# Graph network on one core: edge stages with the layer norm on edge partitions, four buffers, sums and transposes three rounds behind

## What is computed

```python
h = relu(layernorm(x)); x = x + degree_scaled_sum(h[src] -> dst)
e = ln(mlp(edge_attr)); n = ln(mlp(relu(layernorm(x))))
for s in range(2):
    e = e + ln(mlp([e, n[senders], n[receivers]]))
    agg = segment_sum(e, receivers)
    n = n + ln(mlp([n, agg]))
return x + mlp(n)
```

## Time and profile before

| | |
|---|---|
| median of 3 executions | 13500.32 us (13497.44 to 13505.08) |
| profiled execution, first to last instruction | 13501.9 us |
| TensorE busy, mean granted clock | 10188.2 us (75%), 0.851 |
| ScalarE / VectorE / GpSimd busy | 7395.3 / 5621.3 / 9021.1 us |

### The profile page before, as it was taken

How to read it: one execution, slowest core, us unless ns; L and a number is a source line. 1 busy time by engine, 2 the same in 40 slices (tenths; PEclk the granted TensorE clock), 3 DMA queues, 4 the chain that set the end, 5 groups by cost and what they waited for, 6 DMA issues and landing times. The chain is left out here.

```text
span 13501.9 us, 245430 instructions
## 1 busy us (share of the span) xinstructions
PE 10188.2 (75%) x61106; PEld 7311.0 (54%) x61106; DVE 5621.3 (42%) x18295; ACT 7395.3 (55%) x11725; POOL 9021.1 (67%) x9433
## 2 busy tenths in 40 slices
PE   4877777777777777777777777777777777777777
PEld 3655555555555555555555555554555555555554
DVE  5653333333333334444444444443444444444443
ACT  0025555555555535666666666665666666666665
POOL 0037777777777736777777777773777777777773
PEclk9986666666666658999999999998999999999998
DMA  2012222222222223333333333332222333333331
GB/s 76 11 27 43 43 43 43 42 43 43 43 43 43 43 33 82 93 94 94 94 94 94 94 94 93 94 94 58 68 68 68 68 68 68 68 69 68 68 69 33
DMA packets 1693848, 867.49 MB, mean 64 GB/s; under 512 B 1234324, under 2 KB 1391253, under 8 KB 1693347
## 3 DMA queue, kind: packets, MB, share of 16 engines
q1 hardware_dynamic: 1390930, 589.01, 16.6%
q0 software_dynamic: 301056, 257.50, 11.7%
q10 hardware_dynamic: 1808, 20.32, 0.5%
HBM read 635.66 MB, written 246.07 MB: 65 GB/s over the span
## 5 line engine op out<-in xcount | busy, mean ns | idle before, releaser
L1151 POOL DMA_INDIRECT edge_blk_g<-sender_part,edge_blk_idx x6272 | 6014.8, 959 | 2441.7 <-issue 1997.8
L892 POOL DMA_INDIRECT fl_g<-sender_x,fl_idx x3136 | 2992.8, 954 | 1025.9 <-issue 992.3
L1203 PE MATMUL edge_blk_hps<-ident,edge_blk_g 128*128 128x128 f32 x6272 | 1081.6, 325 | 1635.5 <-DMA edge_blk_g<-sender_part,edge_blk_idx 1635.3
L1203 PEld LDWEIGHTS edge_blk_hps<-ident,edge_blk_g 128*128 128x128 f32 x6272 | 910.5, 223 | 2284.9 <-DMA edge_blk_g<-sender_part,edge_blk_idx 2284.0
L1231 ACT ACT_TABLE_LOAD x1568 | 2011.7, 1283 | 51.6 <-PEq L66 23.6
L1276 DVE TENSOR_TENSOR edge_blk_t<-edge_blk_yb,edge_blk_rps 128x512 f32<-128x512 f32 x784 | 539.5, 688 | 2420.5 <-PE edge_blk_rps L1167 2420.3
L1237 ACT ACTIVATE edge_blk_h<-edge_blk_hps,vecs 128x512 f32<-128x512 f32 x784 | 538.8, 687 | 1485.5 <-PE edge_blk_hps L1203 1483.1
L1244 ACT ACTIVATE edge_blk_sq<-edge_blk_yps,vecs 128x512 f32<-128x512 f32 x784 | 538.9, 687 | 1388.7 <-PE edge_blk_yps L1211 1384.1
L984 ACT ACTIVATE fl_sq<-fl_yps,vecs 128x512 f32<-128x512 f32 x392 | 269.4, 687 | 1641.2 <-PE fl_yps L947 1641.2
L1308 DVE TENSOR_SCALAR edge_blk_ohb<-row_f,edge_blk_lst 128x64 f32<-128x64 f32 x6272 | 1115.7, 277 | 6.4
L975 ACT ACT_TABLE_LOAD x784 | 1005.9, 1283 | 31.5 <-PEq L66 17.5
(11 more groups left out here) (222 smaller groups left out, 15503.1 us busy)
## 6 DMA issues: line engine op xcount, KB each, us to landing
edge_blk_e<-edge_state SPq DMA_DIRECT2D x784, 256.0 KB
edge_state<-fl_e SPq DMA_DIRECT2D x392, 256.0 KB
edge_blk_dlb<-local_dst SPq DMA_DIRECT2D x1568, 64.0 KB
edge_blk_g<-sender_part,edge_blk_idx POOLq DMA_INDIRECT x6272
edge_state<-edge_blk_new SPq DMA_DIRECT2D x392, 256.0 KB, 2.1
fl_g<-sender_x,fl_idx POOLq DMA_INDIRECT x3136
edge_blk_win<-receiver_part SPq DMA_DIRECT2D x1568, 16.0 KB
fl_attr<-attr_slots SPq DMA_DIRECT2D x392, 32.0 KB
```

The lines of the kernel that those rows point to most:

```text
L892: pool.indirect_dma_start(out=g[n.b][:, j, :], out_offset=None, in_=xg_d, in_offset=bass.IndirectOffsetOnAxis(ap=idx[n.b][:, j:j + 1].bitc ...
L1151: pool.indirect_dma_start(out=g[n.b][:, i, 64 * c:64 * c + 64], out_offset=None, in_=ps_d, in_offset=bass.IndirectOffsetOnAxis(ap=idx[n.b] ...
L1203: ins = nc.tensor.matmul(h_ps[:, P * i:P * i + P], g[n.b][:, i, :], ident[:, :], start=False, stop=i == TILES - 1)
```

## The change

Each edge round keeps its gathers and its three products, and changes what follows `h`:

- `y` is computed with `h` as the stationary operand (`second`), so that the edges lie on partitions. The bias is a row (`b1_row`), added by VectorE (`yb`); ScalarE squares `yb` from SBUF; VectorE reduces, inverts and multiplies. The matmuls `varps` and `rps` and ScalarE's `rs_x`, `yb` and `eb` are gone.
- The sums use the normalized `t` directly. Gain is applied as they are added, and `agg` is not cleared in the edge steps: it carries over, and `agg_w` and a corrected bias of `edge_blk1` carry the gains' and offsets' part for the nodes. The edge state in HBM leaves out the offset in the steps.
- `sums` and `turn` (transposes of `t`; in the first layer by 64-wide matmuls) run three rounds behind, in the first layer four.
- Buffers filled by loads, `t`, `new` and `ohb` are fourfold, PSUM outputs double. Index list and receiver list are one load. `rounds` unrolls four rounds.
- `ohb` is one broadcast `tensor_tensor` and no longer eight `tensor_scalar`; the first layer's `e` is a `tensor_scalar` from PSUM.

The first layer's gathered rows land beside `t` in `gx`, and one set of matmuls sums both (96 columns). The setup gets some sixteen small VectorE operations and eight matmuls. Cut to its core:

```diff
 edge_step, GpSimd:
-  landed(pool, idx_in, n)
-  wait(pool, pre, n.back(2))
+  landed(pool, list_in, n)
+  wait(pool, pre, n.back(4))
 edge_step, VectorE:
-  for j in range(8):
-      ins = v.tensor_scalar(ohb[n.b][:, j, :], row_f[:, 0:WIN], lst[n.b][:, j:j + 1].bitcast(F32), None, ALU.is_equal)
+  v.tensor_tensor(ohb[n.b][:, :, :], row_f[:, 0:WIN].rearrange("p (j w) -> p j w", j=1).broadcast_to([P, 8, WIN]),
+                  lst[n.b][:, 8:16].bitcast(F32).rearrange("p (j w) -> p j w", w=1).broadcast_to([P, 8, WIN]), ALU.is_equal).then_inc(ohb_ok, 1)
-  v.tensor_tensor(t[:, :], yb[n.b][:, :], r_ps[:, :], ALU.mult).then_inc(t_ok, 1)
-  v.scalar_tensor_tensor(new[n.b][:, :], t[:, :], col("g"), eb[n.b][:, :], ALU.mult, ALU.add).then_inc(new_ok, 1)
+def normed(n):
+  wait(dve, y_ok, n)
+  v.tensor_tensor(yb[n.half][:, :, :], y_ps[n.half][:, :].rearrange("p (j d) -> p j d", d=D),
+                  b1_row.rearrange("p (j d) -> p j d", j=1).broadcast_to([P, 8, D]), ALU.add).then_inc(yb_ok, 1)
+  wait(dve, sq_ok, n)
+  v.tensor_reduce(red[:, :], sq[:, :, :], AX_X, ALU.add).then_inc(red_ok, 1)
+  wait(dve, sd_ok, n)
+  v.reciprocal(rs[:, :], sd[:, :]).then_inc(r_ok, 1)
+  wait(dve, r_ok, n)
+  v.tensor_tensor(t[n.b]..., yb[n.half][:, :, :], rs[:, :]...broadcast_to([P, 8, D]), ALU.mult).then_inc(t_ok, 1)
+def finish(n):
+  v.scalar_tensor_tensor(new[n.b][:, :], t_ps[n.half][:, :], col("g"), e[n.b][:, :], ALU.mult, ALU.add).then_inc(new_ok, 1)
+def body(n):
+  one_hots(n)
+  add_sums(n.back(3))
+  finish(n.back(3))
+  normed(n.back(1))
-  v.memset(agg[:, :], 0.0).then_inc(zeroed, 1)
+  for b in range(QUAD):
+      ins = v.memset(win[b][:, :], 0.0)
+  ins.then_inc(zeroed, 1)
 edge_step, TensorE:
+def second(n):
+  wait(pe, h_ok, n)
+  wait(pe, yb_ok, n.back(2))
+  for i in range(TILES):
+      ins = nc.tensor.matmul(y_ps[n.half][:, P * i:P * i + P], h[n.half][:, P * i:P * i + P], w_mid[:, :], start=True, stop=True)
+  ins.then_inc(y_ok, 1)
 def body(n):
+  sums(n.back(3))
+  turn(n.back(3))
+  second(n.back(1))
   ...
 edge_step, ScalarE:
+def body(n):
+  scale(n.back(1))
+  silu(n)
 edge_step, SP:
+def body(n):
+  indices(n)
+  operands(n.back(2))
+  store(n.back(6))
 first_layer, TensorE and VectorE:
+for i in range(TILES):
+  for c in range(2):
+      ins = nc.tensor.matmul(t_ps[n.half][64 * c:64 * c + 64, P * i:P * i + P], gx[n.b][:, i, c, 0:D], ident[:, :], start=True, stop=True)
 def body(n):
-  encode(n.back(1))
-  turn_in(n)
-  spread_out(n.back(2))
-  sums(n.back(2))
-  second(n.back(1))
+  second(n.back(2))
+  encode(n.back(1))
+  turn_in(n)
+  sums(n.back(4))
+  turn(n.back(4))
 def body(n):
+  attr_copy(n)
+  one_hots(n.back(2))
+  normed(n.back(2))
+  add_sums(n.back(4))
+  finish(n.back(4))
 finish(n):
-  v.tensor_scalar(e[n.b][:, :], t[:, :], col("g"), col("beta"), ALU.mult, ALU.add).then_inc(e_ok, 1)
+  v.tensor_scalar(e[n.b][:, :], t_ps[n.half][:, :], col("g"), col("beta"), ALU.mult, ALU.add).then_inc(e_ok, 1)
```

More of the change, by code:

```diff
@@ L835, in first_layer @@
         sem = ctx.enter_context(semaphores(nc, "fl_"))
[L837 to L844, removed]
-        rs_x = two("rs_x", [P, 2 * TILES, D])
-        yb = two("yb", [P, CHUNK])
@@ L847, in first_layer @@
-        idle = sb("idle", [P, 1])
-        e = two("e", [P, CHUNK])
-        at_ps, h_ps, var_ps, agg_ps, r_ps = ps("atps"), ps("hps"), ps("varps"), ps("aggps"), ps("rps")
-        y_ps = [ps("yps0"), ps("yps1")]
-        idx_in, list_in, attr_in, g_in, e_out = ([sem(f"{k}{i}") for i in range(2)] for k in ("idx_in", "list_in", "attr_in", "g_in", "e_out"))
+        lst = many(QUAD, "lst", [P, 16], I32)
+        attr = many(QUAD, "attr", [P, 8, E_DIM])
+        gx = many(QUAD, "gx", [P, TILES, 2, D + XG])
@@ L956, in body, with turn @@
+                def turn(n):
+                    if not n.exists():
+                        return
+                    wait(pe, e_ok, n.back(2))
+                    for i in range(TILES):
+                        for c in range(2):
+                            ins = nc.tensor.matmul(t_ps[n.half][64 * c:64 * c + 64, P * i:P * i + P], gx[n.b][:, i, c, 0:D],
+                                                   ident[:, :], start=True, stop=True)
+                    ins.then_inc(turned, 1)
                 def body(n):
+                    second(n.back(2))
@@ L967, in _ @@
-                second(last.back(1))
-                spread_out(last.back(1))
-                sums(last.back(1))
+                for k in (4, 3, 2, 1):
+                    sums(last.back(k))
+                    turn(last.back(k))
+                    if k == 4:
+                        second(last.back(1))
             @block.scalar
@@ L999, in _ @@
+                last = rounds(act, body, count_sb, 2)
+                scale(last.back(2))
+                silu(last.back(1))
+                scale(last.back(1))
             @block.vector
@@ L1090, in edge_step @@
-        rs_x = two("rs_x", [P, 2 * TILES, D])
-        yb = two("yb", [P, CHUNK])
-        idle = sb("idle", [P, 1])
-        new = two("new", [P, CHUNK])
-        new_t = sb("new_t", [P, TILES, P])
-        y_ps = [ps("yps0"), ps("yps1")]
-        h_ps, var_ps, t_ps, agg_ps, r_ps = ps("hps"), ps("varps"), ps("tps"), ps("aggps"), ps("rps")
-        idx_in, list_in, dlb_in, win_in, g_in, e_in, e_out = (
-            [sem(f"{k}{i}") for i in range(2)] for k in ("idx_in", "list_in", "dlb_in", "win_in", "g_in", "e_in", "e_out"))
+        lst = many(QUAD, "lst", [P, 16], I32)
@@ L1192, in body @@
+                def second(n):
+                    if not n.exists():
+                        return
+                    wait(pe, h_ok, n)
+                    wait(pe, yb_ok, n.back(2))
+                    for i in range(TILES):
+                        ins = nc.tensor.matmul(y_ps[n.half][:, P * i:P * i + P], h[n.half][:, P * i:P * i + P], w_mid[:, :],
+                                               start=True, stop=True)
+                    ins.then_inc(y_ok, 1)
                 def body(n):
-                    wait(pe, h_ok, n.back(1))
@@ L1219, in body @@
[L1219 to L1225 removed]
+                last = rounds(pe, body, count_sb, 2)
+                for k in (3, 2, 1):
+                    sums(last.back(k))
+                    turn(last.back(k))
+                    if k == 3:
+                        second(last.back(1))
             @block.scalar
```

575 lines of the change are left out of this document (280 added, 295 removed).

## The result

The changed kernel takes 13600.13 us (median of 4 runs, 13591.66 to 13606.61) against 13500.01 us of the kernel before (4 runs): ratio 1.0072, 95% interval 1.0058 to 1.0087. It is slower by 0.7%, where 13402 us was forecast.

What follows compares the result with a forecast made beforehand. POOL's gathers with their issue were taken as the bound, 11732 of the loops' 12019 us. Terms -5 - 83 - 25 + 5 + 7 + 3 = -98 us on 13501.9 gave 13404, as median 13402 us; range 13340 to 13500.

Steps and rivals of the forecast that it cites:

- POOL as the bound: In the three loops, POOL's gathers and their issue set the time: 11732 of 12019 us, other engines' work fitting beside them.
- -83: Stretched gathers in the three loops: 35, 28 and 20 us won by the new `ohb` and `fl_e` from PSUM.
- The second rival: New two-input VectorE operations in the loops disturb gathers, 62 ns at each of 2352 places: +145 us, 13547; chance 0.05.
- The first rival: Nothing won on gathers: `oha`, placed elsewhere in VectorE's round, costs what `ohb` cost: 13485 us, no change; chance 0.08.
- the fourth: Rival: all disturbance of gathers in the loops goes, -160 us, 13340; chance 0.05.
- The pauses: POOL's pauses at one in 112 gathers, 142 us in the loops, were expected to stay: no change.
- The clearing: Before the two edge steps, `agg` no longer cleared lets SP's first load start earlier: twice -12.5, -25 us.
- the tails of the first two stages: Last sums, turns and store after the last gathers grow: +7 us in the first layer, +3 in `edge_blk0`.
- The waits: POOL waiting in the loops for rounds four before instead of two takes away only what was waited: -5 us.
- Setup: Before the loops, some sixteen small VectorE operations and eight matmuls behind the last weight: +5 us, between 3 and 10.
- End of `edge_blk1`: The last edge step stores nothing, so its deeper tail was priced at 0 us.
- The third rival: The first layer's round outgrows POOL's 10.2 us at low TensorE clock: 11.4 us a round, 13870 us; chance 0.08.

Runs made afterwards that it cites:

- run 8: The kernel after, first edge step held to two rounds of gathers under way, second with its list in two transfers: 14294.47 us, ratio 1.0584.
- run 12: The kernel after with `ohb` built by eight `tensor_scalar`s a round in place of one `tensor_tensor`: 13461.68 us, ratio 0.9971 to the kernel before.
- run 5: The kernel after with one input of `ohb` and of the norm's multiply in PSUM, for one `h` or sum bank less: 13285.04 us, ratio 0.9834.
- run 6: The kernel of run 5 with `oha` also made a `tensor_tensor` with one input in PSUM: 13248.22 us, ratio 0.9808 to the kernel before.
- run 9: The kernel before with `ohb` as one `tensor_tensor` of two SBUF inputs in place of eight `tensor_scalar`s: 13597.32 us, ratio 1.0072.
- run 10: The kernel before with `ohb` as one `tensor_tensor` reading its row numbers from PSUM: 13492.06 us, ratio 0.9994.
- run 7: The kernel after with `ohb` alone reading its row numbers from PSUM, the multiplies still reading SBUF twice: 13421.85 us, ratio 0.9936 to the kernel before.
- run 13: The kernel before with four gather buffers and semaphores, four-round loops on SyncE, TensorE and POOL, POOL's wait four rounds back: 13414.71 us, ratio 0.9937.
- run 4: The kernel before with POOL's loop alone written out for four rounds: 17057.81 us with late transfers, ratio 0.9975.
- run 14: The kernel of run 13 with POOL's wait left at two rounds back: 13427.59 us, ratio 0.9946 to the kernel before.
- run 15: The kernel before without the clearing of `agg` ahead of the two edge steps: 13469.46 us, ratio 0.9978.

## Why the prediction was wrong

**POOL as the bound: right**, but for the first edge step of run 8, in every run without late transfers. The excess accounts for the times: run 12 against the kernel after -139 and -138 us, run 5 -310 and -315, run 6 -343 and -352.

**The step that failed** is "A gather that has the whole start of `new` (two inputs in SBUF, 0.75 us) inside it takes 0.94", from which I took two-input operations as harmless: the new `ohb` and the multiplies stood at 0 in the sum, and -83 was left for the gathers. It was +235, and the new operations' own part is 194 + 138 = 332. The row was read without its order in time: at 6003.14 the gather starts, and `new` 0.26 us later, when the gather can no longer be held. I compared an operation that came second with `tensor_scalar`s that came first, and took the difference for one of kind. At 7263.60 the same trace has `new` first and a gather of 1.31 us, and so it is at 5154.19, in the very row that I read as the eight `ohb`. Two wrong shares hid in the -83: `ohb` was given in the edge steps what `new` cost. What the change took away came to 91 to 96 us all the same: `fl_e` 29, `new` 38 (its first input is in PSUM now), the eight `ohb` 5 to 10, and 19 of `oha`, which stands elsewhere. That this is near 83 is luck.

The Trainium skill, "SBUF — State Buffer", section "SBUF: two separate sides", names both halves: two SBUF inputs against a reading GpSimd instruction, and that whichever starts first holds the other off. Runs 5, 9 and 10 agree with the holding of gathers, at up to 0.53 us a gather in run 9. The other way round the traces agree for `tensor_scalar` alone:

```profile
1160.78 0.94 POOL L892 DMA_INDIRECT fl_g<-sender_x,fl_idx  x1 [0.30 <-issue]
1161.21 0.77 DVE L1019 TENSOR_SCALAR fl_e<-fl_t,vecs 128x512 f32<-128x512 f32 x1
```

is the kernel before; `fl_e` takes 0.55 us elsewhere. `new` takes 0.75 us wherever in a gather it starts, and here the measurement decides against the Trainium skill. The section "Who interferes with whom" of the same page of the Trainium skill infers that `tensor_tensor` would spare the writing of descriptors; whatever part of an indirect gather is held here, the gathers behind `ohb` were held.

**The second rival** had the right mechanism at a chance of 0.05 and the wrong size: 62 ns a place was an average over the old places, and the 332 us over its 2352 new ones are 141 ns. The size hangs on how rounds and gathers stand to one another (run 7: 37 against 104 us), and no sum over places gives that. What the prediction named as its sign came: means over 0.955 us beside `tensor_tensor` operations. The first rival stayed away, `oha` cost 32 us and not 51, and the fourth: no disturbance at all is run 6, not this change.

**The pauses: wrong, the other way.** "The number of gathers stays, so I leave them": the 142 us were gone. The number of gathers was no cause but a count. Four buffers with four semaphores and loops of four on SyncE and TensorE take them away in the kernel before too (run 13); which of these three does it stays open, as does what POOL does in a pause. Its own loop of two rounds is excluded as the cause by run 4 and its wait by run 14, and two list transfers alone don't bring pauses back (run 8's second edge step, run 13).

**The small terms.** The clearing: -25 forecast, -28 in run 15. With the tails of the first two stages (+7 and +3) -15 forecast, -13 read in the two windows between the loops. The waits: -5 forecast, about -4 found (POOL's waits for other engines took 5.2 us beyond the 0.305 of issue each before, 1.2 after). Setup: +5 forecast, the first loop starts at the same 865 us. End of `edge_blk1`: 0 forecast, +17. The node phase behind it runs at another clock:

```profile
13321.00:13501.90 180.90, 144.22 (x644) 79.05 (x643) 44.35 (x194) 99.52 (x146) 0.00 (x0) 0.76 0.07 6
```

is the kernel before, against 197.20 us, 157.90 of TensorE and a clock of 0.67 in the last window after: 14 us more TensorE time in this stretch, where TensorE is on the path. I had forecast the lower clock (0.6 to 0.8 in the edge steps; 0.83 came) and priced it only inside the loops. That the clock makes these 17 us was not tried by itself.

**The third rival** stayed away: TensorE is busy 3227 / 392 = 8.2 us of a first-layer round, and POOL waited for `aggps` 4.6 us in all.

## What to carry to other kernels

Where GpSimd's gathers are the bound, list the VectorE operations of the loop by where their inputs lie, and give each one of two SBUF inputs, and each `tensor_scalar` from SBUF to SBUF, one operand in PSUM: a constant, or a column just computed. (The `tensor_reduce` from SBUF needed none of it: 449 gathers of the kernel after began 0.2 us or more before the end of one, and none took over 0.956 us.) Here that was worth 352 us (2.6%), with `ohb` and the multiplies as long as before and `oha` 0.19 us longer. When a row is used to clear a kind of operation, note which of the two started first, and look for the opposite order before believing it. And a regular loss whose cause is not known is not a constant of the kernel: give its going away a chance of its own.

## What the runs showed of the hardware

- A gather of 0.94 us that starts while a certain VectorE operation runs lasts until the operation's end plus 0.82 us (984 gathers of the kernel after, within 0.04 us). It holds for `tensor_tensor` and `scalar_tensor_tensor` with two SBUF inputs and for `tensor_scalar` from SBUF to SBUF; with one input in PSUM nothing is held (run 6). The limit is not quite the gather's start: by the kind of operation it lies between 0.15 us before it (`fl_e`) and 0.13 us into it (`ohb` of the first layer).
- The reverse is seen for `tensor_scalar` from SBUF to SBUF alone: one that starts 0.43 us into a gather takes 0.77 us and not 0.55, while `new`, with two SBUF inputs, keeps its 0.75 us.
- Pauses of about 2 us come at one gather in 112 or in 96, always before the second gather of a round but wherever this round stands in POOL's loop, and can vanish altogether (142 us with the few waits) without a change to the gathers.
